# 200 slots a batch, deep entries picked apart where rows meet, and picking that starts with the first tile

## What is computed

```python
mask = adj != 0
scores = jnp.where(mask, -jnp.arange(N), -inf)
vals, idx = jax.lax.top_k(scores, 25)          # the first 25 neighbours of each node
feats = jnp.where(valid[..., None], x[idx], -inf)
agg = feats.max(axis=2)                        # their largest value, feature by feature
agg = jnp.where((degree <= 25)[..., None], jnp.maximum(agg, 0.0), agg)
out = relu(concatenate([x, agg], -1) @ W + b)
y = layernorm(x + out)
```

## Time and profile before

| | us |
|---|---|
| median of 3 runs | 624.4 (624.03 to 627.11) |
| the profiled execution, its own time | 624.25 |
| its span, first to last instruction | 622.4 |
| busy in it: DVE / PE / ACT / POOL | 534.3 / 501.3 / 394.6 / 290.4 |
| mean granted TensorE clock | 0.956 |

### The profile page before, as it was taken

The page is one execution under the profiler, slowest core; times in us unless marked ns, Lnnn a source line. Parts: engine busy times, 40 slices in busy tenths (PEclk is TensorE's granted clock), DMA queues, the critical chain, the costliest instruction groups (busy, mean ns, idle before and its releaser), DMA issues.

```text
span 622.4 us, 14481 instructions
## 1 busy us (share of the span) xinstructions
PE 501.3 (81%) x4480; PEld 341.9 (55%) x4544; DVE 534.3 (86%) x973; ACT 394.6 (63%) x751; POOL 290.4 (47%) x462
## 2 busy tenths in 40 slices
PE   1366997889968996889974999679987999779982
PEld 0124675566654675456752666555764567555762
DVE  4656999899898998899995998998898999998884
ACT  3361577448965688557864588665886478545744
POOL 2643365246633655146733356335552467336610
PEclk9997999899998999799997999998999999899996
DMA  8982336353434647345534445355544463021102
GB/s 244 224 221 72 102 98 129 98 153 96 134 95 137 151 115 125 106 130 143 132 97 112 133 107 137 86 141 137 135 124 120 116 141 59 18 57 36 46 10 70
DMA packets 91815, 71.38 MB, mean 115 GB/s; under 512 B 63651, under 2 KB 80294, under 8 KB 91686
## 3 DMA queue, kind: packets, MB, share of 16 engines
q1 hardware_dynamic: 85286, 56.77, 35.6%
q0 software_dynamic: 6400, 13.12, 8.4%
HBM read 50.99 MB, written 4.19 MB: 89 GB/s over the span
## 4 chain that ended last, share of the span: by engine, by line
PE 30%; DVE 22%; issue 14%; ACT 12%; DVEq 8%; DMA 7%; another core or an unknown queue 3%; POOL 1%; SPq 1%; POOLq 1%; ACTq 0%
PE pair L1037 25%; DVE part L776 11%; DMA adj_sb<-in_adj 3%; ACT row_work L712 3%; DMA g_feat<-in_x,g_idx 3%; DVE hot L771 3%; ACT mask L586 3%; DVEq L846 3%; DVEq L915 2%; ACT distance L629 2%; ACT hot L636 2%; DVE g_feat L849 2%; PE misc L1082 1%; DVE g_val L817 1%
## 5 line engine op out<-in xcount | busy, mean ns | idle before, releaser
L1037 PE MATMUL pair<-hot,x_part 128*128 128x128 bf16 (+3 forms) x3120 | 416.6, 281 | 66.0 <-DVE part L776 33.8
L1037 PEld LDWEIGHTS pair<-hot,x_part 128*128 128x128 bf16 x3120 | 239.0, 99 | 176.1 <-issue 64.0
L776 DVE TENSOR_REDUCE part<-pair 128x128 f32<-128x1024 f32 (+1 forms) x256 | 279.8, 1099 | 47.2 <-PE pair L1037 45.9
L484 POOL DMA_INDIRECT g_feat<-in_x,g_idx x200 | 192.8, 964 | 112.5 <-issue 96.0
L521 POOL TENSOR_TENSOR y_sb<-relu_sb,x_sb 128x128 f32<-128x128 f32 x64 | 32.8, 512 | 194.1 <-ACT relu_sb L647 193.8
L593 ACT ACTIVATE V<-p_V 128x512 bf16<-128x512 f32 x98 | 58.0, 592 | 93.4 <-remote 71.7
L621 ACT ACTIVATE hot<-V,first_bias 128x1024 bf16<-128x1024 bf16 x56 | 64.1, 1145 | 52.8 <-PE pair L1037 52.8
L771 DVE TENSOR_SCALAR hot<-V 128x1024 bf16<-128x1024 bf16 x224 | 84.3, 397 | 0.0
L586 ACT ACTIVATE mask<-adj_sb 128x1024 bf16<-128x1024 uint32 x56 | 58.8, 1050 | 20.5 <-DMA adj_sb<-in_adj 20.5
L636 ACT ACTIVATE hot<-distance,one 128x1024 bf16<-128x1024 bf16 x56 | 64.0, 1143 | 0.2
L629 ACT ACTIVATE distance<-V,second_bias 128x1024 bf16<-128x1024 bf16 x56 | 63.7, 1137 | 0.0
(11 more groups left out here) (88 smaller groups left out, 396.6 us busy)
## 6 DMA issues: line engine op xcount, KB each, us to landing
adj_sb<-in_adj SPq DMA_DIRECT2D x56, 512.0 KB
g_adj<-in_adj SPq DMA_DIRECT2D x8, 512.0 KB, 4.4
x_sb<-in_x SPq DMA_DIRECT2D x8, 512.0 KB, 3.9
out<-y_sb SPq DMA_DIRECT2D x7, 512.0 KB, 5.1
g_feat<-in_x,g_idx POOLq DMA_INDIRECT x200
maskT<-mask SPq DMA_TRANSPOSE x56
out<-y_sb SPq DMA_DIRECT2D x1, 448.0 KB, 3.0
w_sb<-in_W SPq DMA_DIRECT2D x1, 128.0 KB, 6.3
```

Source lines behind the costliest of these rows:

```text
L484: pool.indirect_dma_start(out=g_feat[w][:, k, :], out_offset=None, in_=x_rows, in_offset=bass.IndirectOffsetOnAxis(ap=g_idx[w][:, k:k + 1] ...
L776: dve.tensor_reduce(part[:, par(q, s), :, p], slots_of(q, s, p).rearrange("f k i -> f i k"), AX.X, ALU.max).then_inc(s_used, 1)
L1037: last = pe.matmul(dst, x_part[:, q, part_no, kb], one_hot, start=(first and part_no == 0), stop=(final and part_no == PARTS - 1))
```

## The change

- The slots of a step are dealt anew: more entries share, three shared slots a step instead of two or three, runs are split so that every bank is full. Every group has 8 slots: 5 groups in step 1, 4 in steps 2 and 3, 3 in steps 4 to 7, which is 25 groups and 200 slots a batch. The shared slots and what is left are always in the last group.
- A new level bit (`APART`, 2): where two entries of a shared slot meet in a row, the tile is no longer redone. The last group's five own slots are reduced again, and the 15 shared entries are picked once more, each into a slot of its own, behind the step (`apart_level`, `apart_reduce`). The redo becomes level 4.
- Only tile 1 is prepared ahead of the first pick. Batch 0 prepares two tiles a step (`to_prepare`), so that it catches up to the distance of seven; its levels come in three passes (steps 1, 3 and 4), its own tile 0 is extracted during its first two steps, and its gathers are in steps 3 to 5, nine a step. The first split of `x` moves from POOL to DVE.

Core of the diff:

```diff
-SHARED = {1: (((0, 11), (3, 5), (4, 6), (5, 5), (7, 5)), ((0, 12), (1, 7), (3, 6), (4, 5), (6, 5))),
-          2: (((0, 9), (1, 5), (2, 5), (3, 5), (4, 5), (6, 5)), ((1, 6), (5, 5), (6, 4), (7, 4))),
-          4: (((0, 7), (1, 5), (2, 4), (4, 4), (5, 4), (6, 4), (7, 4)), ((3, 4), (5, 3)), ((6, 3), (7, 3)))}
+SHARED = {1: (((0, 12), (2, 6), (3, 5), (4, 6), (7, 4)), ((0, 10), (1, 6), (5, 5), (6, 5), (7, 5)),
+              ((0, 11), (1, 7), (3, 6), (4, 5), (6, 4))),
+          2: (((1, 6), (2, 4), (6, 4)), ((0, 8), (2, 5), (3, 5), (4, 4), (5, 4), (7, 4)),
+              ((0, 9), (1, 5), (3, 4), (4, 5), (5, 5), (6, 5))),
+          4: (((0, 7), (1, 5), (2, 4), (3, 4), (4, 3), (6, 4), (7, 3)), ((0, 6), (4, 4), (5, 3), (6, 3)),
+              ((1, 4), (3, 3), (5, 4), (7, 4)))}
...
+        def to_prepare(i, q, s):
+            if is_first(i, q):
+                return [(0, n // MT, n % MT + 1) for n in (2 * s - 1, 2 * s) if n < 2 * MT]
+            t = ahead(i, q, s, FRONT)
+            return [t] if t else []
+        def levels_at(i, q, s):
+            return ({1: (1, 2), 3: (3, 5), 4: (6, MT)} if is_first(i, q) else {1: (1, MT)}).get(s)
...
             load_adj0(0, 0)
             load_adj(0, 0, 1)
+            load_x(0, 0)
+            transpose_mask(0, 0, 1)
             load_adj(0, 0, 2)
-            load_x(0, 0)
...
-            transpose_mask(0, 0, 1)
-            for n in range(2, FRONT + 3):
-                sp.wait_ge(s_mask, n - 1)
-                load_adj(*ahead(0, 0, 1, n))
-                if n <= FRONT + 1:
-                    transpose_mask(*ahead(0, 0, 1, n - 1))
+            load_adj(0, 0, 3)
+            transpose_mask(0, 0, 2)
+            load_adj(0, 0, 4)
...
 # POOL
-                if s == 1:
+                first, each = (3, -(-K // 3)) if is_first(i, q) else (1, GATHER)
+                if s == first:
...
 # ACT, step
+                    if early:
+                        copy_V(*a, 0)
+                        copy_V(*a, 1)
                     if nxt:
                         first_rank(*nxt)
                         second_distance(*nxt)
...
+                    if a and not early:
+                        copy_V(*a, 0)
                     if nxt:
                         second_rank(*nxt)
+                    if b and not early:
+                        copy_V(*a, 1)
+                    if a and ahead(*a, 2):
+                        make_mask(*ahead(*a, 2))
...
+                    if b:
+                        copy_V(*b, 0)
+                        copy_V(*b, 1)
+                        make_mask(*ahead(*b, 2))
+                    elif a:
+                        copy_V(*a, 1)
                     if s > 1:
                         relu(i, q, s - 1)
...
 # ACT, ahead of the first step
+            split_high(0, 0)
             make_mask(0, 0, 2)
+            split_mid(0, 0)
+            act.wait_ge(s_Vp, 1)
+            nc.scalar.activation(V[:, 0, 0, 0:BANK], pairs[1][:, 0:BANK], ACT.Copy).then_inc(s_V, 1)
...
 # DVE
+            def apart_reduce(i, q, s):
+                dve.wait_ge(s_used, pair_no(i, q, s, COUNT[s]))
+                dve.tensor_reduce(part[:, par(q, s), :, COUNT[s] - 1], buffer_of(q, s, COUNT[s] - 1)[:, 0:OWN_LAST]
+                                  .rearrange("f k i -> f i k"), AX.X, ALU.max)
+                for p in range(EXTRA):
+                    dve.wait_ge(s_xpair, 2 * EXTRA * pos(i, q, s) + p + 1)
+                    dve.tensor_reduce(more[:, :, p], apart_slots(q, s, p).rearrange("f k i -> f i k"),
+                                      AX.X, ALU.max).then_inc(s_xused, 1)
+                dve.drain()
+                maxima = part[:, par(q, s), :, 0:EXTRA]
+                dve.tensor_tensor(maxima, maxima, more[:, :, :], ALU.max).then_inc(s_xdone, 1)
...
+                dve.scalar_tensor_tensor(out=unlike[:, :], in0=vsum[:, LEVELS], scalar=float(APART), in1=vsum[:, 0],
+                                         op0=ALU.mult, op1=ALU.add)
+                dve.drain()
...
+            FIRST_STEPS = {(1, 0): 3, (1, 1): 4, (1, 2): 5, (1, 3): 6, (1, 4): 7, (2, 0): 8}
...
 # PE, step
                     pick_group(i, q, s, 0)
+                    if a:
+                        rank_product(*a, 0)
                     pick_group(i, q, s, 1)
+                    if b:
+                        rank_product(*a, 1)
+                    if a and (begin or s > 1) and not levels_now:
+                        out_free(i, q, ORDER[s - 1] if s > 1 else 0)
+                        count(*a)
+                    pick_group(i, q, s, 2)
+                    if levels_now:
+                        violations(i, q, s)
+                        pe.wait_ge(s_level, level_pass(i, q, s))
+                        pe.nop(nofuse=True)
+                        out_free(i, q, ORDER[s - 1])
+                        count(*a)
...
+                    if a:
+                        rank_product(*(b or a), 0 if b else 1)
                     for p in range(4, COUNT[s]):
                         pick_group(i, q, s, p)
+                    if b:
+                        rank_product(*b, 1)
...
+            def apart_level(i, q, s):
+                u = par(q, s)
+                for p in range(EXTRA):
+                    pe.wait_ge(s_used, pair_no(i, q, s, COUNT[s]))
+                    members = MEMBERS[s][2 * BANK * p:2 * BANK * (p + 1)]
+                    for k, (kb, r) in enumerate(members):
+                        one_hot = hot[:, u, r - 1, kb] if r <= LOW else hot_high[:, u, r - 1 - LOW, kb]
+                        pick(apart_slots(q, s, p)[:, k], q, kb, one_hot, s_xpair if k == len(members) - 1 else None)
```

More of the change, by code:

```diff
@@ L65, in banks @@
     assert sum(own) + len(taken) == sum(depths)
[L66 to L82, removed]
+    runs = sorted(((kb, r, min(BANK, d - r)) for kb, d in enumerate(own) for r in range(0, d, BANK)), key=lambda run: -run[2])
+    count = -(-(sum(own) + len(shared)) // BANK)
+    filled = [[]]
+    free = [BANK - len(shared)]
+    while runs:
+        kb, r, n = runs.pop(0)
+        home = next((h for h in range(len(filled)) if free[h] >= n), None)
+        if home is None and len(filled) < count:
+            filled.append([])
+            free.append(BANK)
+            home = len(filled) - 1
+        if home is None:
+            home = max(range(len(filled)), key=lambda h: free[h])
+            runs.insert(0, (kb, r + free[home], n - free[home]))
+            n = free[home]
+        used = BANK - free[home] - (len(shared) if home == 0 else 0)
+        for a, z in ((r, min(r + n, LOW)), (max(r, LOW), r + n)):
+            if a < z:
+                filled[home].append((kb, a, z - a, used + a - r))
+        free[home] -= n
+    for j, slot in enumerate(shared):
+        filled[0] += [(kb, r - 1, 1, BANK - len(shared) + j) for kb, r in slot]
     return filled
@@ L88, in groups @@
     filled = banks(depths, shared)
[L89 to L93, removed]
+    filled = sorted(filled[1:], key=lambda bank: max(r + n for kb, r, n, place in bank)) + filled[:1]
+    return [[(kb, r, n, BANK * h + place) for h, bank in enumerate(filled[g:g + BANKS])
+             for kb, r, n, place in bank] for g in range(0, len(filled), BANKS)]
 def build(nc, x, adj, W, b, out):
@@ L111, in build @@
     assert FRONT == MT
+    MEMBERS = {s: [member for slot in SHARED[s] for member in slot] for s in SHARED}
+    assert all(len(MEMBERS[s]) <= EXTRA * 2 * BANK and len(SHARED[s]) == SHARES for s in SHARED)
     SLOTS = {s: [max(n + place for kb, r, n, place in group) for group in GROUPS[s]] for s in GROUPS}
@@ L494, in gather0 @@
                         wait(s_g0max, 2 * i + q)
-                gather(0, s_g0, range(GATHER * (s - 1), min(GATHER * s, K)))
+                gather(0, s_g0, range(max(each * (s - first), 0), max(min(each * (s - first + 1), K), 0)))
             def redo(i, q, s):
                 m = pos(i, q, s)
-                if s == 1:
-                    wait(s_level, 2 * i + q + 1)
-                lv = pool.value_load(level[0:1, q, s - 1:s], min_val=0, max_val=LEVELS)
-                with pool.If(lv == LEVELS):
+                if levels_at(i, q, s):
+                    wait(s_level, level_pass(i, q, s))
+                lv = pool.value_load(level[0:1, q, s - 1:s], min_val=0, max_val=REDO)
+                with pool.If(lv == REDO):
                     pool.dma_start(g_adj[1][:, :], adj_tiles[bass.ds(2 * NT * i + NT * q + s, 1)]
@@ L868, in redo @@
                     last = dve.tensor_copy(part[:, par(q, s), :, p], p_xt)
[L869 removed]
+                last.then_inc(s_xdone, 2)
             def merge(i, q, s):
@@ L929, in step @@
                     nxt = (i, q, s + 1) if s < MT else None if last else (ni, nq, 1)
-                    steps = {} if last else EXTRACT[s]
+                    steps = {} if last else FIRST_EXTRACT[s] if begin else EXTRACT[s]
                     gaps = COUNT[s] - 1
@@ L1121, in step @@
                     if s in (*TURNS, MT):
```

(2 more changed lines are left out.)

247 lines of the change are left out of this document (132 added, 115 removed).

## The result

The changed kernel takes 661.8 us (median of 4 runs, 660.6 to 663.9) where the kernel before takes 624.95 (4 runs): ratio 1.059 [1.0545, 1.063], 36.9 us slower. The prediction, 613.5 (597 to 628), was wrong in sign.

The account below looks back on a forecast made before the run. DVE and PE, both near full, bound it in turns: PE paces steps 3 to 5, DVE steps 6, 7 and 1. Span 622.4 - 30.5 (groups) + 9.6 (start, batch 0) + 10 (two tiles) = 611.5; time 613.5, range 597 to 628.

Parts of the forecast that it names:

- Start: Before the first pick: preparing less there brings the first pick at 18.3 instead of 38.05 us, -19.7.
- Step 1: Batch 0, step 1: work left out of the start makes it take 32.7 us for 22.9, +9.8.
- Batch 0, steps 2 to 7: Two tiles a step through one bank, paced by PE and ACT: 80.8 us against 61.3, +19.5.
- a rider of +15: Batch 0: if half-clock picks come too, start and batch 0 net about +15 instead of +9.6.
- rival D: Batch 0: steps of 14 us instead of 11, PE at half clock between halves, 18 more, 631.5; chance 0.10.
- Fewer, fuller groups: All batches: 25 groups instead of 32 shorten DVE's work, 4.5 us a batch gained, -30.5 in all.
- rival C: Batch loop: PE becomes the bound, its long last group starves DVE, period falls only 1.5, 634 us; chance 0.15.
- Batch 7: Last batch: prepares nothing and waits on PE in the middle, so the groups gain only 3.5 us.
- Meeting tiles: Tiles where shared entries meet: 5 us each (4.2 to 6.5) for the two after batch 0, +10.
- Rival E: PE's picks: narrow matmuls do not hide weight loads, up to 7.2 us a batch, 668 in all; chance 0.05.
- Gathers: Step 6: DVE waits 0.77 us for tile 0's gathers; with the change, more than 0.8 a batch.
- A to E: Five outcomes: the forecast (606 to 620) 0.42, handshakes hidden or PE warm (594 to 606) 0.28, then 0.15, 0.10, 0.05.

Follow-up runs that it names:

- h1: Changed kernel with shared entries dealt so that no rows meet, and the start and batch 0 of the kernel before: 614.3 us, ratio 0.988 to the kernel before.
- f3: Changed kernel with ACT doing the previous tile's ReLU ahead of the second tile's copies and mask in batch 0: 648.4 us, ratio 1.035 to the kernel before.
- i2: Kernel before with tile 0's gathers issued seven a step, in four steps instead of five: 611.3 us, ratio 0.984 to the kernel before.
- i1: h1 with tile 0's gathers issued seven a step, in four steps instead of five: 599.1 us, ratio 0.961 to the kernel before.
- f2: Changed kernel with the shared entries dealt so that no rows meet and nothing is picked apart: 634.5 us, ratio 1.0135 to the kernel before.
- f4: Kernel before with picks cut to at most 2 slots, 132 more matmuls and weight loads a batch: 632.3 us, ratio 1.014 to the kernel before.

## Why the prediction was wrong, point by point

Put in the terms that the runs can tell apart, the prediction's sum was -30.5 for the groups, -1.5 for start and batch 0 without meeting tiles, and +21 for the four tiles (6.6, 4.5, 5, 5): -11. The runs gave -10.2, +20.6 and +27.1: +37.5 (2.9 of the 10.2 fall in batch 0, where the prediction counted no gain of the groups; h1's check of batch 1 comes at 119.40 for 122.25). The first two terms failed, each by some 20 us; the third was right in kind and 6 too small.

- **Start, -19.7: right.** First picks at 18.48 for a predicted 18.3. **Step 1, +9.8: too dear.** Step 2 began at 47.25, not 51.0; the extra picks ran warm (45 matmuls in 2.7 us for 4.8, the 24 of the extra ranks in 2.79 for 5.30). The sum also leaves out the 1.3 that its text has for the one-hots; with it, its own terms end at 52.3.
- **Batch 0, steps 2 to 7: failed, 20.8 us short** (101.6 for 80.8). The prediction named `p_V`'s copies, which hold PE 5.1 us. It missed that `count` waits for the ReLU queued behind them, which ACT's and PE's loops in the diff, read side by side, show: worth 13.2 us, half of it clock (f3). Its 4.4 us for ACT's queue are also more than the parts that it names, which add to 4.0 with the ReLU's 0.27 of rows 6. About 1 us more is the meeting tile. Some 7 us, mostly in steps 3 and 4 with their level passes, were not tested; in the trace PE waits 4.7 us for DVE in those passes (1.9 for the counts, 2.8 for the levels), where the prediction named about 1.5 in step 3. The half-clock picks stood in the text as a rider of +15, and as rival D; its point, a check from about 145 on, was met at 148.9.
- **Fewer, fuller groups, 4.5 a batch: failed, 1.2 measured.** DVE's work did fall by 4.4. The step that failed is "In steps 6, 7, 1 and 2 DVE holds or PE restarts behind it", which let four steps' shorter reductions through to the end. In merge-to-merge times, means over batches 1 to 6, before against h1, step 2 went from 10.5 to 9.4 (1.1 gained, predicted 1.4) and steps 3 to 5 from 25.3 to 25.1 (0.3 for 1.2), but steps 6, 7 and the next step 1 together from 35.9 to 36.1, where 2.2 were to be gained; with seven gathers a step, from 34.1 to 34.2 (i2, i1). Three places show in the traces: the restart behind the level check (1.3 a batch lost for 0.7 gained), step 6 with its gathers (1.0 a batch, see above), and one collision of DVE and POOL, told below (0.5 a batch). DVE and PE took turns in these steps, and PE became the one that is waited for. That is rival C, with its period falling by 1.5 and its test (DVE's idle time growing as its work shrinks: 19.2 of 26.6). Its 634 is what f2 took, by luck: f2 holds batch 0's excess as well.
- **Batch 7, 3.5 gained: 0.3** in h1 (68.8 for 69.15). It was counted on waits for PE in the middle, which stayed.
- **Meeting tiles: mechanism right, 6.8 each for 5.3.** Missing were PE's wait for DVE to catch up first (4.1 in batch 7) and 0.7 us from DVE's maximum to PE's next matmul. The 45 matmuls took 4.1, within the text's 2.5 to 4.8.
- **Rival E: refuted at its price.** 423 more matmuls a batch cost 8.0 us in all, where 55 were put on 129. A cost of some 7 us, as f4 has for 132, is not excluded. The rule of the Trainium skill (TensorE: Matmul & The Clock Gate, Back-to-back issue gap), 81 ns in such a stream, does not fit either: 56 measured, in streams of 42.
- **Gathers: the wait was read right** (11.4 us in eight batches, over 0.8 each) and its use missed. The earlier trace rows showed DVE waiting 0.77 for transfers that one constant could start a step sooner, worth 11.9 us by i2: more than the groups.
- **The chances.** A to E were treated as alternatives. C and D happened together, and the tile price was short as well: 613.5 + 20.5 + 18 + 6 = 658. With several unproven gains in one change the rivals add, and the range has to hold two of them at once.

## What to carry to other kernels

When two engines are both near full, price work removed from one at zero until a run of the other shows slack: here 26.6 us less on DVE gave 7.4. When a stage is doubled up, write out each queue of that stage in order and ask of every wait in it what stands ahead of its releaser; here taking out waits of up to 1.8 us saved 5.9 us of TensorE's idle time and 6.5 of its busy time, through the clock. A small first group behind a point where all engines wait starts them sooner than a full one (3.6 us for 5.0). A path for rare cases that all engines must meet in costs the meeting (3.7 to 8.2 us a tile here), not the 2.5 us of its matmuls.

## What the runs showed of the hardware that was not expected

- TensorE's clock doubled the price of batch 0's waits (5.9 us of idle time, 6.5 of slower work): PE busy 72.1 us at a granted 0.85 and 65.7 at 0.92 for the same 694 matmuls.
- The kernel before took 623 to 625 us in four jobs, the first included, and 677 to 688 in two. In those two TensorE's picks stood still for 64 to 90 us, for nothing that the profile shows, in kernels with the new groups (16 to 27 in the other jobs; up to some 7 us of either are the loop's head, the last point here). The same edit was 1.6% faster in one kind of job and 2.7% slower in the other, each with an interval clear of 1. Such ratios are only worth carrying with the time of the base kernel beside them.
- POOL's work can hold DVE. In batch 4, step 5, of h1 two bf16 one-hot instructions of DVE take 3.81 us, with 3.30 us of POOL's split of `x` in the same stretch, and end 0.3 behind it. Overlap alone does not do it: in batch 2 the same two take 0.99 in the middle of a split. The step is 10.3 us long for 7.4 in batches 1 to 3, and the kernel before, in which POOL's split met other instructions, has 8.15 there. The same shows in i1, i2, f2 and the changed kernel; no run moved the split.

```profile
371.61 3.81 DVE L817 TENSOR_SCALAR hot<-V 128x1024 bf16<-128x1024 bf16 x2
...
371.84 3.30 POOL L509 TENSOR_TENSOR x_rest<-x_sb,x_part 128x128 f32<-128x128 f32 x8
```

- In all kernels one step at the end of batch 3 is some 4 to 6 us longer than in the batches around it (15.2 for 10.6 and 10.2 before, 14.8 for 9.8 in i1), where PE and DVE go back to the head of the loop over batch pairs. The Trainium skill (Runtime: NRT & Kernel Launch, Instruction fetch mechanics) says that a taken branch out of the window already fetched makes the engine wait for a fetch. The place fits; no run here moved the loop.
